# A 128-column memset, and a wait for it, ahead of each table look-up from the thirteenth tile on

## The chip, the cores and the metric

The kernel runs on one core of a Trainium2 chip. The metric is the device time in microseconds (us) of one execution; lower is better. Times in the text are in us unless ns is written.

## What is computed

A recommendation tower for a batch of 1,024 samples. Each sample looks up 32 embedding rows of 64 numbers, one in each of 32 tables. For each of the 496 pairs of fields, one embedding goes through that pair's own 64x64 matrix and is multiplied and summed with the other embedding. The 496 sums and 16 dense features pass three small layers.

```python
e = jnp.stack([tbl_0[ids[:, 0]], ..., tbl_31[ids[:, 31]]], axis=1)      # (1024, 32, 64)
p, q = e[:, ROW], e[:, COL]                                             # the 496 pairs
z = jnp.sum(jnp.einsum('bpj,ipj->bpi', p, kernel) * q, axis=-1)
h = jnp.concatenate([z, dense_ctx], axis=1)
h = jnp.maximum(h @ W_top1 + b_top1, 0.0)
h = jnp.maximum(h @ W_top2 + b_top2, 0.0)
y = h @ W_top3
```

All of it is in float32.

## The kernel before, in words

**Tiles.** The batch is cut into four blocks of 256 samples, the 32 fields into 16 tiles of two fields. So there are 64 tiles, numbered `m` = 0 to 63, sixteen to a block. A tile of one block is 256 samples x 128 numbers (two fields of 64). Tiles 0, 1 and 4 are not looked up by GpSimd (TensorE makes them by a product with one-hot rows), the other 61 are.

**Look-ups.** GpSimd runs one long loop over the tiles (L401 on). A tile takes four look-ups, one for each of two groups of 128 samples and each of two fields. Each is an indirect DMA (L419) that fetches 128 rows of 64 numbers into `nat` (a ring of eight tiles) or `nat01` (the first two tiles of a block). That is 244 look-ups in all. Before a look-up GpSimd may wait for semaphores: for `transposed` (the ring's slot was read by TensorE, once for each tile), and for `u_ready` and `summed`, which count TensorE's progress. The numbers for these last two come from a plan (`PLAN.in_front`), and ask for work that TensorE does some seven and a half tiles ahead of the tile's own turn. They hold GpSimd back from running further ahead; they are the gates of the text below.

**TensorE.** Its order is written out by the class `Plan` ahead of time and doesn't change with what arrives first. It turns a tile (L644, `transpose`: two or, from the second block on, four matmuls against `ident`) once its look-ups have landed (`gathered`). ScalarE copies the result to `rows` (L492). Then come the pieces of the pair work that need this tile: `interact` (L690 and L697) and `interact_pass` (L711), each 8 or 4 matmuls. VectorE multiplies each piece with the other embedding (L607, L618), ScalarE sums some of them (L504), and TensorE sums the others (`add_up`, L724 and L730). From block 1 on tiles are turned two at a time, as pairs 16/17, 18/19, up to 62/63. TensorE waits at L644 if a pair has not landed, and everything behind it in its order waits too. When the last pair is turned, the rest of the pair work and the three layers (L771, L791, L799) follow.

**The look-up next to other GpSimd work.** Apart from the look-ups GpSimd runs only the set-up at the start: a memset of `ident` (L395), an affine select that waits for it (L397), and an iota (L399).

Of the kernel before, what the change touches and what calls it, by code (L numbers as in the profile page):

```python
# [8 lines left out]
P = 128  # L9
# [94 lines left out]
def tile_at(m):  # L104
    b, tile = divmod(m, TILES)
    return b, FRONT[tile] if b == 0 and tile < len(FRONT) else tile
# [16 lines left out]
def lane_count(m):  # L123

    return 32 * SUBS * (m // LANES + (m % LANES not in BY_PRODUCT))
# [2 lines left out]


AHEAD = 30  # L130


def pieces_in_front(m):
    return max(0, (4 * m - AHEAD) * (ND + NP) // (4 * TILES))

# [9 lines left out]
class Plan:  # L145
# [90 lines left out]
    def in_front(self, m, part):  # L236

        first, last = (next(mark[0] for mark in self.marks if mark[1] == n * (ND + NP)) for n in (1, BLOCKS))
        due = first + (last - first) / (4 * (LOOKED_UP - TILES)) * (4 * (m - TILES) - AHEAD + part)
        return max(mark for mark in self.marks if mark[0] <= max(0, due))  # L240
# [54 lines left out]
def tower(nc, ids, first_ids, tables, kern, dense, w1, b1, w2, b2, w3, out):  # L295
    f32, f32r, u32 = mybir.dt.float32, mybir.dt.float32r, mybir.dt.uint32
    ALU, ACT = mybir.AluOpType, mybir.ActivationFunctionType
    with ExitStack() as ctx:
        def sb(name, shape, dt=f32):
            return ctx.enter_context(nc.sbuf_tensor(name, shape, dt))  # L300
# [4 lines left out]
        def sem(name):  # L305
            return ctx.enter_context(nc.semaphore(name))
# [18 lines left out]
        ident = sb("ident", [P, P])  # L325
        row_number = sb("row_number", [P, CHUNKS])
        sel = sb("sel", [P, 62])


        w1_sb, w2_sb = rows[:, :, 0:P], rows[:, 0:HID1 * HID2 // P // P, P:2 * P]  # L330
# [34 lines left out]
        def h_ps(n):  # L365
            return u_flat[:, n % 6, :]

        ids_in, ident_zero, ident_ready = sem("ids_in"), sem("ident_zero"), sem("ident_ready")
        row_number_ready, ones_ready = sem("row_number_ready"), sem("ones_ready")
        distance_ready, ones_by_act = sem("distance_ready"), sem("ones_by_act")  # L370
# [13 lines left out]
        def nat_of(m, s):  # L384

            b, tile = tile_at(m)
            return nat01[:, b % 2, s, tile, :] if tile < 2 else nat[:, m % RING, s, :]
# [5 lines left out]
        @block.gpsimd  # L393
        def _(pool):
            nc.gpsimd.memset(ident[:], 0.0).then_inc(ident_zero, 1)  # L395
            pool.wait_ge(ident_zero, 1)
            nc.gpsimd.affine_select(out=ident[:], in_=ident[:], compare_op=ALU.not_equal, fill=1.0, base=0,  # L397
                                    pattern=[[-1, P]], channel_multiplier=1).then_inc(ident_ready, 1)
            nc.gpsimd.iota(row_number[:], [[1, CHUNKS]], base=0, channel_multiplier=CHUNKS,  # L399
                           allow_small_or_imprecise_dtypes=True).then_inc(row_number_ready, 1)  # L400
            pool.wait_ge(ids_in, 16)  # L401
            for m in range(LOOKED_UP):
                if m in BY_PRODUCT:
                    continue
                b, tile = tile_at(m)
                if m >= LANES:
                    pool.wait_ge(transposed, m - LANES + 1)
                if tile == 0 and b >= 2:
                    pool.wait_ge(prod_ready, AT[b - 2, None, NP - 1] + 1)
                for n in range(SUBS):  # L410
                    for h in range(2):
                        _, pieces, quads = PLAN.in_front(m, 2 * n + h)
                        if pieces:
                            pool.wait_ge(u_ready, pieces)
                        if quads:
                            pool.wait_ge(summed, quads)
                        f = 2 * tile + h
                        col = (b * SUBS + n) * FIELDS + f
                        pool.indirect_dma_start(  # L419
                            nat_of(m, n)[:, h * EMBED:(h + 1) * EMBED], None, tables[f],  # L420
                            bass.IndirectOffsetOnAxis(ids_sb[:, col:col + 1], 0)).then_inc(gathered[m % LANES], 16)
            for m in range(LOOKED_UP - LANES, LOOKED_UP):
                pool.wait_ge(gathered[m % LANES], lane_count(m))
# [428 lines left out]
```

## Time and profile before

| | |
|---|---|
| time, median of 3 runs | 498.26 us |
| lowest and highest of the runs | 494.0 and 500.97 us |
| span of the profiled execution (first to last instruction) | 412.5 us |
| busy in that span: TensorE (PE) | 403.7 us, 98% |
| busy: VectorE (DVE), ScalarE (ACT), GpSimd (POOL) | 298.6, 259.1, 231.6 us |

The span runs from the first to the last instruction on the engines. The measured time also holds what lies around it, 498.26 - 412.5 = 85.8 us if the profiled execution was like the others. A busy TensorE is one whose matmuls lie back to back in the records; their ends are modelled. A look-up's busy time is GpSimd's part in it (making the descriptors of the transfer), not the transfer.

### The profile page before, as it was taken

Reading aid. Unit: us, or ns where it says so; the run is one execution under the profiler, and the core shown is the slowest. Engines: PE = TensorE matmul, PEld = TensorE weight load, DVE = VectorE, ACT = ScalarE, POOL = GpSimd, SP = SyncE. Lnnn points to the kernel's source line nnn. Section 1 sums busy time; section 2 is a strip of 40 time slices with the busy share of each in tenths; the row PEclk is TensorE's granted clock in tenths of the full one; section 3 lists DMA queues with packets and bytes.
Section 4 is the critical chain, followed back from the end, with each engine's and each line's share of the span. In section 5 each row is a group of like instructions: output and inputs, shape, how many; then the busy total and the mean of one; then the engine's idle time right before and its main releaser. Section 6 shows DMA issues by size and latency. Waiting matters only on the chain.

```text
span 412.5 us, 10180 instructions
## 1 busy us (share of the span) xinstructions
PE 403.7 (98%) x3421; PEld 254.4 (62%) x3421; DVE 298.6 (72%) x293; ACT 259.1 (63%) x1874; POOL 231.6 (56%) x251
## 2 busy tenths in 40 slices
PE   7889999999999999999999999999999999999997
PEld 5556656667675766666766665666666566654442
DVE  6776887878788887878979798878879888740000
ACT  6476877667577876764796867719978667002221
POOL 6777777777677757776766777677767200000000
PEclk9998999999999999999999999999999999999999
DMA  6665661131281111211211113111311020000000
GB/s 177 210 200 155 191 221 33 27 77 27 37 219 28 29 19 47 61 28 25 63 42 28 25 25 79 24 27 26 79 25 27 15 51 2 2 2 0 2 0 1
DMA packets 18266, 24.31 MB, mean 59 GB/s; under 512 B 6387, under 2 KB 11767, under 8 KB 17958
## 3 DMA queue, kind: packets, MB, share of 16 engines
q1 hardware_dynamic: 10406, 15.64, 13.0%
q0 software_dynamic: 7808, 8.01, 9.7%
q8 instruction: 28, 0.46, 0.4%
q14 instruction: 24, 0.20, 0.2%
HBM read 19.44 MB, written 0.00 MB: 47 GB/s over the span
## 4 chain that ended last, share of the span: by engine, by line
PE 92%; DMA 3%; POOL 3%; issue 1%; ACT 0%
PE u_ps L690 41%; PE z_ps L724 14%; PE u_ps L711 13%; PE z_ps L730 7%; PE u_ps L771 7%; PE t_ps L644 4%; PE u_ps L791 3%; POOL nat L419 3%; DMA nat<-tbl,ids_sb 2%; PE u_ps L697 2%; DMA ids_sb<-ids 1%; PE t_ps L677 0%; PE u_ps L799 0%; ACT y_sb L571 0%
## 5 line engine op out<-in xcount | busy, mean ns | idle before, releaser
L419 POOL DMA_INDIRECT nat<-tbl,ids_sb x244 | 230.5, 945 | 90.7 <-issue 56.6
L607 DVE TENSOR_TENSOR prod<-u_ps,rows 128x1024 f32<-128x1024 f32 x184 | 213.5, 1218 | 56.7 <-PE u_ps L690 56.7
L504 ACT ACTIVATE pass_prod<-pass_prod 128x64 f32<-128x64 f32 x896 | 214.3, 243 | 22.1 <-DVE pass_prod L618 22.1
L690 PE MATMUL u_ps<-rows,k_sb 64*128 64x256 f32 x1472 | 176.2, 387 | 0.0
L504 ACT ACTIVATION_READ_ACCUMULATOR pass_prod<-pass_prod 128x1 f32 x896 | 169.9, 190 | 0.0
L690 PEld LDWEIGHTS u_ps<-rows,k_sb 64*128 64x128 f32 x1472 | 139.0, 188 | 46.0 <-DVE pass_prod L618 13.4
L618 DVE TENSOR_TENSOR pass_prod<-u_ps,nat 128x1024 f32<-128x1024 f32 x56 | 67.2, 1215 | 1.2 <-PE u_ps L711 1.2
L711 PE MATMUL u_ps<-k_sb,rows 64*128 64x256 f32 x448 | 61.5, 394 | 0.6 <-ACT rows L492 0.6
L724 PE MATMUL z_ps<-prod,sel 128*32 128x512 f32 x512 | 61.6, 598 | 0.0
L492 ACT ACTIVATE rows<-t_ps 128x512 f32<-128x512 f32 (+1 forms) x38 | 19.6, 516 | 54.2 <-PE t_ps L644 54.0
L711 PEld LDWEIGHTS u_ps<-k_sb,rows 64*128 64x128 f32 x448 | 40.6, 186 | 14.6 <-DVE prod L607 9.6
L730 PE MATMUL z_ps<-prod,sel 128*32 128x256 f32 x512 | 30.7, 382 | 0.0
L724 PEld LDWEIGHTS z_ps<-prod,sel 128*32 128x32 f32 x512 | 13.4, 109 | 27.1 <-issue 24.5
L771 PE MATMUL u_ps<-zT,rows 128*128 128x512 f32 x64 | 27.7, 594 | 0.0
L644 PE MATMUL t_ps<-ident,nat 128*128 128x128 f32 x122 | 21.4, 289 | 3.4 <-DMA nat<-tbl,ids_sb 2.8
L730 PEld LDWEIGHTS z_ps<-prod,sel 128*32 128x32 f32 x512 | 15.1, 109 | 12.5 <-issue 2.7
L644 PEld LDWEIGHTS t_ps<-ident,nat 128*128 128x128 f32 x122 | 12.7, 141 | 16.3 <-issue 11.5
L771 PEld LDWEIGHTS u_ps<-zT,rows 128*128 128x128 f32 x64 | 12.1, 190 | 15.2 <-issue 15.2
L562 ACT ACTIVATE k_sb<-u_ps,b_sb 128x512 f32<-128x512 f32 x8 | 5.5, 687 | 22.4 <-PE u_ps L771 22.4
L791 PE MATMUL u_ps<-k_sb,rows 128*128 128x512 f32 x32 | 13.9, 592 | 0.0
L610 DVE TENSOR_TENSOR prod<-u_ps,by_self 128x1024 f32<-128x1024 f32 x8 | 9.8, 1220 | 5.5 <-PE u_ps L697 5.5
L791 PEld LDWEIGHTS u_ps<-k_sb,rows 128*128 128x128 f32 x32 | 6.1, 190 | 7.7 <-issue 7.7
(50 smaller groups left out, 78.9 us busy)
## 6 DMA issues: line engine op xcount, KB each, us to landing
by_self<-rows SPq DMA_DIRECT2D x32, 128.0 KB
nat<-tbl,ids_sb POOLq DMA_INDIRECT x244
k_sb<-kern SPq DMA_DIRECT2D x3, 768.0 KB, 5.6
k_sb<-kern SPq DMA_DIRECT2D x2, 640.0 KB, 5.7
k_sb<-kern SPq DMA_DIRECT2D x1, 1152.0 KB, 5.2
k_sb<-kern SPq DMA_DIRECT2D x2, 512.0 KB
rows<-w SPq DMA_DIRECT2D x1, 1024.0 KB, 6.6
rows<-tbl SPq DMA_DIRECT2D x4, 224.0 KB
```

Of the source, the lines that this page charges most:

```text
L419: pool.indirect_dma_start(nat_of(m, n)[:, h * EMBED:(h + 1) * EMBED], None, tables[f], bass.IndirectOffsetOnAxis(ids_sb[:, col:col + 1], 0 ...
L492: nc.scalar.activation(rows[:, tile:tile + count, cols_of(b)], t_ps[:, 0:count].rearrange("p t n c -> p t (n c)"), ACT.Copy).then_inc(rows ...
L504: op = nc.scalar.activation(of, of, ACT.Copy, accum_out=z_nat[:, b % 2, s, row:row + 1])
L607: nc.vector.tensor_tensor(to, u, by.unsqueeze(1).to_broadcast([P, 2, 2, SIZE]), ALU.mult).then_inc(prod_ready, 1)
L618: nc.vector.tensor_tensor(pass_prod[:, k % CRING], u, by.to_broadcast([P, 2, 2, SIZE]), ALU.mult).then_inc(prod_ready, 1)
L644: op = nc.tensor.transpose(t_ps[:, t, s, :], nat_of(m + t, s), ident[:])
L690: op = nc.tensor.matmul(u[:, h, :], k_sb[part, k_of(d), side, :], rows[part, tile, cols_of(b)], start=True, stop=True)
L711: op = nc.tensor.matmul(u_ps[:, n % URING, h, t, :], rows[part, first + t, at:at + P], k_sb[part, k].rearrange("p s n -> p (s n)"), start= ...
L724: op = nc.tensor.matmul(z_ps[32 * k:32 * k + 32, :, :], sel[:, 30 - 2 * slot:62 - 2 * slot], prod[:, (a + k // 2) % PRING, k % 2], start=s ...
L730: op = nc.tensor.matmul(z_ps[32 * k:32 * k + 32, 0, :], sel[:, 30 - row:62 - row], prod[:, (a + k // 2) % PRING, k % 2, side], start=slot ...
L771: op = nc.tensor.matmul(h_ps(n), w1_sb[:, r * (HID1 // P) + m, :], zT[:, r, cols], start=r == 0, stop=r == ZROWS - 1)
L791: op = nc.tensor.matmul(h_ps(8 + n), w2_sb[:, g * (HID2 // P) + m, :], h1T(g, cols), start=g == 0, stop=g == HID1 // P - 1)
```

## The change

A new tensor `zeros` (128 x 128 float32) and a new semaphore `zeros_there` are added. For tiles with `m >= 12`, in front of each look-up and behind the gates of that look-up, GpSimd writes zeros into `zeros` and waits until that write is complete. Nothing reads `zeros`. Tiles 2, 3 and 5 to 11 (36 look-ups) stay as they were; tiles 12 to 63 (52 tiles, 208 look-ups) have the memset and the wait.

```diff
+SPACED = 12
...
+        zeros = sb("zeros", [P, P])
...
+        zeros_there = sem("zeros_there")
...
                         if quads:
                             pool.wait_ge(summed, quads)
+                        if m >= SPACED:
+                            nc.gpsimd.memset(zeros[:], 0.0).then_inc(zeros_there, 1)
+                            pool.wait_ge(zeros_there, 4 * (m - SPACED) + 2 * n + h + 1)
                         f = 2 * tile + h
                         col = (b * SUBS + n) * FIELDS + f
                         pool.indirect_dma_start(
```

**Where the spacing starts.** The rows below are GpSimd's own instructions in program order around the border from tile 11 to tile 12. A row is the line, the operation, what it writes and reads, the semaphores it waits for, and a count of like instructions in a row. Before:

```order
L419 DMA nat<-tbl,ids_sb 128x64 [waits summed,u_ready,transposed]
L419 DMA nat<-tbl,ids_sb 128x64 [waits summed,u_ready] x3
L419 DMA nat<-tbl,ids_sb 128x64 [waits summed,u_ready,transposed]
L419 DMA nat<-tbl,ids_sb 128x64 [waits summed,u_ready] x3
L419 DMA nat<-tbl,ids_sb 128x64 [waits summed,u_ready,transposed]
L419 DMA nat<-tbl,ids_sb 128x64 [waits summed,u_ready] x3
```

And of the changed kernel (L419 is now L425, the memset is L421):

```order
L425 DMA nat<-tbl,ids_sb 128x64 [waits summed,u_ready,transposed]
L425 DMA nat<-tbl,ids_sb 128x64 [waits summed,u_ready] x3
L421 MEMSET zeros 128x128 [waits summed,u_ready,transposed]
L425 DMA nat<-tbl,ids_sb 128x64 [waits zeros_there]
L421 MEMSET zeros 128x128 [waits summed,u_ready]
L425 DMA nat<-tbl,ids_sb 128x64 [waits zeros_there]
L421 MEMSET zeros 128x128 [waits summed,u_ready]
L425 DMA nat<-tbl,ids_sb 128x64 [waits zeros_there]
L421 MEMSET zeros 128x128 [waits summed,u_ready]
L425 DMA nat<-tbl,ids_sb 128x64 [waits zeros_there]
```

The gates now stand on the memset, and the look-up waits for the memset alone. Before, a look-up whose gates were open had nothing to wait for.

**Block starts.** The same holds further on, at the first tile of the third block, whose look-up had four waits. Here the rows carry the tables' numbers. Before:

```order
L419 DMA nat01<-tbl_0,ids_sb 128x64 [waits u_ready,summed,prod_ready,transposed]
L419 DMA nat01<-tbl_1,ids_sb 128x64 [waits summed,u_ready]
L419 DMA nat01<-tbl_0,ids_sb 128x64 [waits summed,u_ready]
L419 DMA nat01<-tbl_1,ids_sb 128x64 [waits summed,u_ready]
L419 DMA nat01<-tbl_2,ids_sb 128x64 [waits summed,u_ready,transposed]
```

Of the changed kernel:

```order
L421 MEMSET zeros 128x128 [waits u_ready,summed,prod_ready,transposed]
L425 DMA nat01<-tbl_0,ids_sb 128x64 [waits zeros_there]
L421 MEMSET zeros 128x128 [waits summed,u_ready]
L425 DMA nat01<-tbl_1,ids_sb 128x64 [waits zeros_there]
L421 MEMSET zeros 128x128 [waits summed,u_ready]
L425 DMA nat01<-tbl_0,ids_sb 128x64 [waits zeros_there]
```

No look-up has changed its place among the look-ups, and TensorE, VectorE, ScalarE and SyncE have the same instructions in the same order as before.

## Rows read from the trace of the kernel before

**Rows 1.** The page: busy time, and the chain that ended last by engine

```profile
PE 403.7 (98%) x3421; PEld 254.4 (62%) x3421; DVE 298.6 (72%) x293; ACT 259.1 (63%) x1874; POOL 231.6 (56%) x251
PE 92%; DMA 3%; POOL 3%; issue 1%; ACT 0%
```

**Rows 2.** Windows (start:end, length, busy of each engine), two stretches

```profile
core 0: us, PE busy (x) PEld busy (x) DVE busy (x) ACT busy (x) POOL busy (x), PEclk, DMA share, GB/s
48.50:332.60 284.10, 284.10 (x2634) 186.27 (x2630) 236.93 (x207) 205.54 (x1586) 196.18 (x208) 1.00 0.22 50
332.60:412.50 79.90, 77.29 (x480) 40.44 (x478) 27.55 (x24) 21.69 (x111) 0.00 (x0) 1.00 0.03 8
```

**Rows 3.** GpSimd's groups by line: busy us, mean ns, idle before, releasers

```profile
L419 POOL DMA_INDIRECT nat<-tbl,ids_sb x244 | 230.5, 945 | 90.7 <-issue 56.6 <-PE u_ps L690 16.3 <-PE z_ps L724 5.7
```

**Rows 4.** Timeline of GpSimd: tile 11's last look-ups, tile 12's first

```profile
start us, us, engine line op out<-in xcount [idle before <-releaser]
45.99 0.94 POOL L419 DMA_INDIRECT nat<-tbl,ids_sb  x1 [0.30 <-PE u_ps L711]
47.24 0.95 POOL L419 DMA_INDIRECT nat<-tbl,ids_sb  x1 [0.30 <-issue]
48.49 0.94 POOL L419 DMA_INDIRECT nat<-tbl,ids_sb  x1 [0.31 <-issue]
49.73 0.95 POOL L419 DMA_INDIRECT nat<-tbl,ids_sb  x1 [0.30 <-PE u_ps L690]
```

**Rows 5.** The same: last look-up of tiles 17, 59 and 63

```profile
77.20 0.94 POOL L419 DMA_INDIRECT nat<-tbl,ids_sb  x1 [0.30 <-issue]
...
300.80 0.96 POOL L419 DMA_INDIRECT nat<-tbl,ids_sb  x1 [0.31 <-PE u_ps L697]
...
322.22 0.94 POOL L419 DMA_INDIRECT nat<-tbl,ids_sb  x1 [0.55 <-issue]
```

**Rows 6.** Timeline of TensorE: where pairs 16/17, 58/59 and 62/63 are turned

```profile
88.17 0.66 PE L644 MATMUL t_ps<-ident,nat 128*128 128x128 f32 x4
...
305.30 0.66 PE L644 MATMUL t_ps<-ident,nat 128*128 128x128 f32 x4
...
332.65 0.65 PE L644 MATMUL t_ps<-ident,nat 128*128 128x128 f32 x4
```

**Rows 7.** Tile 3: its last look-up, and the weight load (PEld) that waited for it

```profile
12.28 0.94 POOL L419 DMA_INDIRECT nat<-tbl,ids_sb  x1 [0.30 <-issue]
15.63 0.20 PEld L644 LDWEIGHTS t_ps<-ident,nat 128*128 128x128 f32 x2 [0.77 <-DMA nat<-tbl,ids_sb]
```

**Rows 8.** Chain that ended last: two look-ups from start to landing

```profile
17.27 5.88 DMA nat<-tbl,ids_sb
27.26 4.41 DMA nat<-tbl,ids_sb
```

**Rows 9.** Timeline of GpSimd at the start: set-up and first two look-ups

```profile
0.74 0.20 POOL L395 MEMSET ident<- 128x128 f32 x1 [0.29 <-POOLq L808]
1.19 0.64 POOL L397 TENSOR_SCALAR_AFFINE_SELECT ident<-ident 128x128 f32<-128x128 f32 x1 [0.24 <-POOL ident L395]
1.79 0.13 POOL L399 IOTA row_number<- 128x8 f32 x1
3.22 1.27 POOL L419 DMA_INDIRECT nat<-tbl,ids_sb  x1 [1.29 <-DMA ids_sb<-ids]
4.80 0.94 POOL L419 DMA_INDIRECT nat<-tbl,ids_sb  x1 [0.30 <-issue]
```

**Rows 10.** GpSimd's groups again: the set-up's memset, 128 columns

```profile
L395 POOL MEMSET ident<- 128x128 f32 x1 | 0.2, 204 | 0.3 <-POOLq L808 0.3
```

**Rows 11.** Windows: before, in and after a fall of the clock (PEclk)

```profile
26.40:31.70 5.30, 3.26 (x28) 2.44 (x26) 5.23 (x5) 4.22 (x35) 4.08 (x5) 1.00 0.64 183
33.00:36.50 3.50, 3.50 (x21) 2.84 (x20) 2.45 (x2) 3.50 (x31) 2.59 (x4) 0.51 0.55 128
36.50:48.50 12.00, 12.00 (x110) 6.82 (x108) 9.24 (x8) 8.76 (x70) 8.95 (x11) 1.00 0.75 239
```

## The prediction

> **What bounds the kernel now.** I read the page first: TensorE is busy for 98% of the span, and the chain that ended last is 92% TensorE [rows 1]. Then I cut the span in two by windows. Up to 332.6 us GpSimd still looks rows up, and TensorE is busy in every microsecond; behind it come 79.9 us of TensorE work with no look-up left [rows 2]. So TensorE bounds the kernel, and the look-ups cost nothing as long as each pair of tiles has landed by its turn.
>
> How much room is there? The mean share of GpSimd (56%) misleads. A look-up is busy for 0.945 us [rows 3], but back-to-back look-ups start 1.25 us apart, 0.94 busy and 0.30 between [rows 4]. From the first look-up of tile 12 (48.49) to the last of tile 63 (322.22) there are 207 intervals [rows 4, 5]: 273.7 / 207 = 1.322 us each. At full speed they would be 1.25 us. So GpSimd is at 95% of what it can issue, and only 15 us in this stretch are waits for gates. This is the number on which the change falls.
>
> The deadline of each pair is in TensorE's timeline: pairs 16/17, 58/59 and 62/63 are turned at 88.17, 305.30 and 332.65, with nothing waited for [rows 6]. From 16/17 to 62/63 there are 23 steps: 244.5 / 23 = 10.6 us for eight look-ups, 1.33 us for one.
>
> How long after its start can a look-up be used? Tile 3's last one starts at 12.28 and the weight load that waited for it starts at 15.63, which is 3.35 us [rows 7]; two others in the busy early part took 5.88 and 4.41 [rows 8]. Pair 58/59 was turned 4.5 us after its last look-up started, without a wait [rows 5, 6], so it took at most that. I take 3.4 us, because the DMA queues are much quieter later on (share 0.22 against 0.64 [rows 2, 11]). The cushion is then 88.17 - 77.20 - 3.4 = 7.6 us at pair 16/17, 305.30 - 300.80 - 3.4 = 1.1 us at pair 58/59 and 332.65 - 322.22 - 3.4 = 7.0 us at the last pair.
>
> **The change, part by part.** Nothing is removed, and TensorE's order is the same. Added are 208 memsets and 208 waits, all on GpSimd. The only things queued behind the memset are the look-ups, and TensorE waits for these at L644.
>
> The price is the new spacing of look-ups. I build it from four parts.
>
> 1. The look-up's own busy time, 0.94 us [rows 4].
> 2. From its end to the start of the memset. The trace has no memset behind a look-up. From below: an instruction that waits for nothing can start before the one ahead has ended; the iota starts at 1.79 while the affine select runs to 1.83 [rows 9]. So 0. From above: the 0.30 us between two look-ups [rows 4]. I take 0.20: the predecessor is that of the upper row, but part of the 0.30 must belong to the start of the second look-up.
> 3. The memset, 0.204 us for the same 128 x 128 shape [rows 10].
> 4. From its end to the look-up that waits for it. The set-up has the same pattern, a memset and an instruction that waits for it: 0.24 us [rows 9]. The 0.30 in front of a look-up is the other bound. I take 0.27. This wait can't be hidden: it is the point of the semaphore.
>
> The sum is 0.94 + 0.20 + 0.20 + 0.27 = 1.62 us (1.61 before rounding up). The ends are 0.94 + 0 + 0.20 + 0.24 = 1.39 and 0.94 + 0.30 + 0.20 + 0.30 = 1.75 us.
>
> One rule bears on step 3. A start-to-start reading of the set-up gives 1.19 - 0.74 = 0.45 us from the memset to the instruction waiting for it [rows 9], against 0.20 + 0.24 = 0.44 as I add it. The Trainium skill (Perfetto Trace Analysis, the part on the GPSIMD engine instruction) says that a GpSimd span is unreliable and should be timed by start-to-start spacing. By that alone the period would be 1.25 + 0.45 = 1.70 us and the time about 570 us; the row agrees with the span to 0.01 us, so this moves only step 2 to its upper end.
>
> Now the schedule. The last unspaced look-up starts at 47.24 [rows 4]. The k-th spaced one starts at 47.24 + 1.62 k if it never waits for a gate. Eight look-ups take 13.0 us where TensorE wants a pair each 10.6 us. Each look-up loses 1.62 - 1.25 = 0.37 us. The cushion of 7.6 us at pair 16/17 is used up after some 20 look-ups, about there; from pair 18/19 on TensorE waits at nearly each pair.
>
> - Tile 59 ends with spaced look-up 4 x 48 = 192: it starts at 47.24 + 311.0 = 358.3 instead of 300.80, 57.5 us later. Less 1.1 us of cushion: TensorE turns the pair 56.4 us later.
> - Tile 63 ends with number 208: 47.24 + 337.0 = 384.2 instead of 322.22, 62.0 us later, less 7.0: 55.0 us. The earlier pair decides.
>
> The gates cost nothing more. They ask for TensorE's work of some seven tiles earlier, and TensorE will stand waiting for the next pair when GpSimd gets to them, so it has done everything ahead of that. The 15 us of gate waits of before vanish into the spacing; the sum above has them, since it goes by start times. The tail of 79.9 us [rows 2] is unchanged and moves as a whole.
>
> So the span goes from 412.5 to 412.5 + 56.4 = 468.9 us. The median of the runs, 498.26, is 85.8 us above the profiled span; the same 56.4 us on it gives 554.7, **555 us**, 11% slower. Each 0.1 us on the spacing is worth 19.2 us.
>
> **The rivals.**
>
> *A: the memset hides, and the time stays.* It runs beside the end of the look-up ahead, and the dependent look-up is dispatched at once. The turning point is where tile 59 uses only its cushion: 47.24 + 192 p = 300.80 + 1.1, p = 1.326 us; up to p = 1.38 the loss is under 10 us, 2%. At 1.326 the time would be 498, at 1.38 some 508 us. For it: GpSimd's starts do overlap once [rows 9]. Against it: even with step 2 at zero, the rows give 1.39. The Trainium skill (GPSIMD Engine Reference, Instruction dispatch) says that consecutive GpSimd instructions are no barrier between its eight cores, and that one instruction's completion waits for all eight. By this most cores could write zeros early, but those that made the descriptors could not, and the wait is for all; so the rule allows step 2 to be short and not the sum to be under 1.39, some 510 us. No row here shows the cores apart.
>
> *B: a look-up behind another kind of instruction starts cold.* The first look-up, behind the iota, was busy for 1.27 us, the second for 0.94 [rows 9]: 0.33 more. If each memset has this effect, the spacing is 1.95 us: 47.24 + 192 x 1.95 = 421.6, 120.8 us later, less 1.1: 119.7, and 618 us. Against it: the first look-up is also the first of the program, and the row can't say which of the two it was.
>
> *C: TensorE falls to its lower clock while it waits.* After a stretch of 5.3 us in which it was busy for 3.26, it ran at a granted clock of 0.51 (1.2 GHz) for 3.5 us, then at 1.00 again [rows 11]. In the changed kernel it idles 2.4 us in every 13.0. If each pair brought one such fall, its 10.6 us of work would grow by some 1.7 us to 12.3, still under 13.0: the waits get shorter and nothing is lost. Only a fall behind the last wait counts, 1.7 us or so. It would have to last through whole pairs to decide, and then there would be no idle time left to cause it. As an addition above 10 us I give it little.
>
> *D: faster.* Look-ups that are further apart could land sooner, or leave more for the other transfers. The transfers behind 48.5 us hold up nothing now [rows 2], so there is nothing to win.
>
> **How the numbers follow.** Chances: the forecast's mechanism with a spacing from 1.39 to 1.80 us 0.82 (510 to 589 us), A 0.05, B 0.10, C as a large addition 0.02, D 0.01. Low end: a spacing of 1.43 gives 47.24 + 274.6 - 300.80 - 1.1 = 19.9, 518 us. High end: 1.82 gives 94.5, 593 us; this is a little above the rows' upper bound, and takes in a small part of B. Beyond these I leave one in ten above and less than one below. About 2% is what a measurement of this kernel can tell from no change. Faster by more than 2%: 0.01; within 2%: 0.05; slower: 0.94.
>
> **What would show it.** In GpSimd's timeline behind 48 us: a memset of 0.20 us in front of each look-up, starts 1.62 us apart (1.39 to 1.75), with idle time of about 0.2 and 0.27 on its two sides, and no gate named as a releaser behind pair 18/19. TensorE waits at L644 for the look-ups' DMA, some 2.4 us at each of about 23 pairs, 56 us in all, and is busy for 86% of the span rather than 98%. The chain that ended last runs through GpSimd from about 50 to 360 or 380 us. The last look-up starts near 384, and the stretch behind the last turn is still about 80 us. I am wrong if look-ups keep their 1.25 us apart, if their busy time changes from 0.94, or if the tail grows.

## The result, and the profile after

In the same comparison the kernel before took 497.15 us and the changed kernel 500.99 us (medians of 20 runs each). The ratio is 1.0067, with a 95% interval from 1.0039 to 1.0096; it is taken from the executions within 1.5% of each kernel's fastest. I had said 555 us, with 518 to 593 as the range. Both the size and the range were wrong: the change costs some 3 to 4 us there and not 57.

The experiments found which step failed, and one fact has to stand first. **Comparisons of this kernel come in two kinds.** A comparison here is one session, in which the kernels run in turn on one chip. In some, every execution of the kernel before takes 488 to 503 us; in others every one takes 411 to 417 us, with nothing between. I call them the long and the short kind. The profile from which I predicted has a span of 412.5 us, so it is of the short kind. The times beside it, 498.26 us as the median, are of the long kind. I took the 85.8 us between them for time that lies around the span. In the changed kernel's profiled run the time is 504.66 us and the span 502.9, so what lies around it is 1.8 us.

The changed kernel in the long kind, its page:

```profile
span 502.9 us, 10388 instructions
PE 438.3 (87%) x3421; PEld 262.3 (52%) x3421; DVE 302.2 (60%) x293; ACT 261.2 (52%) x1874; POOL 277.5 (55%) x459
PE 72%; another core or an unknown queue 10%; DVE 7%; ACT 6%; issue 4%; DVEq 0%; ACTq 0%
L425 POOL DMA_INDIRECT nat<-tbl,ids_sb x244 | 231.7, 949 | 95.5 <-issue 40.0
L421 POOL MEMSET zeros<- 128x128 f32 x208 | 44.7, 215 | 37.2 <-PE u_ps L696 12.9
```

TensorE was 98% busy in [rows 1] and is 87% busy here, as I had expected (86%), and yet not for my reason. The 208 memsets are there, 215 ns each. In front of them GpSimd still waits for TensorE (`u_ps L696`): it is held by the gates, so it is not the bound.

Its spacing where no gate holds it, from GpSimd's timeline:

```profile
67.56 0.95 POOL L425 DMA_INDIRECT nat<-tbl,ids_sb  x1 [0.27 <-POOL zeros L421]
68.52 0.22 POOL L421 MEMSET zeros<- 128x128 f32 x1
69.01 0.95 POOL L425 DMA_INDIRECT nat<-tbl,ids_sb  x1 [0.27 <-issue]
```

Look-ups start 1.44 us apart: 0.95 busy, next to nothing to the memset, 0.22 for it, 0.27 behind it. Before it was 1.25 us [rows 4].

TensorE's waits at the turning of tiles (all of line L650, from the view of one line):

```profile
L650 PE MATMUL t_ps<-ident,nat x122: 272/273/475, 29.2 to 423.4; 128*128 128x128 f32 x122
its engine sat idle before it (us, times) until:
  ACT rows L498: 0.8, 1
```

TensorE never sits idle at a turn for a look-up, where I had forecast 56 us of such waits. The last of these matmuls starts at 423.4. And the cut of the span by windows, which answers to [rows 2]:

```profile
48.50:423.00 374.50, 326.31 (x2756) 201.44 (x2754) 252.33 (x218) 222.06 (x1700) 251.71 (x426) 0.97 0.20 47
423.00:502.90 79.90, 77.30 (x480) 40.45 (x478) 27.53 (x24) 20.44 (x99) 0.00 (x0) 1.00 0.03 8
```

The tail is 79.9 us in both. All of the difference between the kinds lies in the part in which look-ups run, and there TensorE is no longer busy in every microsecond (326.3 of 374.5).

### The profile page after: what moved, and what is told of

Its sections match the earlier page's. It is cut to its first block, busy times and chain, and to the rows that moved or that the text cites. A ratio compares the mean times of both kernels' runs of the same rounds, so it can differ in the third digit from the quotient of the medians.

```text
span 502.9 us, 10388 instructions
## 1 busy us (share of the span) xinstructions
PE 438.3 (87%) x3421; PEld 262.3 (52%) x3421; DVE 302.2 (60%) x293; ACT 261.2 (52%) x1874; POOL 277.5 (55%) x459
## 4 chain that ended last, share of the span: by engine, by line
PE 72%; another core or an unknown queue 10%; DVE 7%; ACT 6%; issue 4%; DVEq 0%; ACTq 0%
PE u_ps L696 31%; PE z_ps L730 12%; PE u_ps L717 12%; DVE prod L613 6%; PE u_ps L777 6%; PE z_ps L736 4%; PE t_ps L650 3%; ACT pass_prod L510 3%; PE u_ps L797 3%; DVE pass_prod L624 1%; PE u_ps L703 1%; PE z_ps L672 1%; ACT rows L498 1%; PE t_ps L683 0%
## 5 line engine op out<-in xcount | busy, mean ns | idle before, releaser
L425 POOL DMA_INDIRECT nat<-tbl,ids_sb x244 | 231.7, 949 | 95.5 <-issue 40.0
L696 PE MATMUL u_ps<-rows,k_sb 64*128 64x256 f32 x1472 | 186.7, 391 | 37.4 <-DVE prod L613 27.8
L696 PEld LDWEIGHTS u_ps<-rows,k_sb 64*128 64x128 f32 x1472 | 138.9, 187 | 94.2 <-DVE prod L613 43.7
L717 PE MATMUL u_ps<-k_sb,rows 64*128 64x256 f32 x448 | 69.3, 436 | 9.3 <-DVE prod L613 6.9
L421 POOL MEMSET zeros<- 128x128 f32 x208 | 44.7, 215 | 37.2 <-PE u_ps L696 12.9
L717 PEld LDWEIGHTS u_ps<-k_sb,rows 64*128 64x128 f32 x448 | 44.8, 208 | 30.2 <-DVE prod L613 18.6
L736 PE MATMUL z_ps<-prod,sel 128*32 128x256 f32 x512 | 34.2, 382 | 1.4 <-issue 1.1
L730 PEld LDWEIGHTS z_ps<-prod,sel 128*32 128x32 f32 x512 | 13.5, 110 | 28.8 <-issue 28.1
L736 PEld LDWEIGHTS z_ps<-prod,sel 128*32 128x32 f32 x512 | 16.4, 109 | 16.0 <-issue 7.1
L650 PE MATMUL t_ps<-ident,nat 128*128 128x128 f32 x122 | 22.6, 299 | 0.9 <-ACT rows L498 0.8
L650 PEld LDWEIGHTS t_ps<-ident,nat 128*128 128x128 f32 x122 | 13.2, 145 | 14.6 <-issue 14.6
L672 PE MATMUL z_ps<-zT,rows 125*64 125x256 f32 x16 | 6.0, 567 | 9.1 <-issue 9.0
```

Source lines behind the costliest of these rows:

```text
L421: nc.gpsimd.memset(zeros[:], 0.0).then_inc(zeros_there, 1)
L425: pool.indirect_dma_start(nat_of(m, n)[:, h * EMBED:(h + 1) * EMBED], None, tables[f], bass.IndirectOffsetOnAxis(ids_sb[:, col:col + 1], 0 ...
L650: op = nc.tensor.transpose(t_ps[:, t, s, :], nat_of(m + t, s), ident[:])
L696: op = nc.tensor.matmul(u[:, h, :], k_sb[part, k_of(d), side, :], rows[part, tile, cols_of(b)], start=True, stop=True)
L717: op = nc.tensor.matmul(u_ps[:, n % URING, h, t, :], rows[part, first + t, at:at + P], k_sb[part, k].rearrange("p s n -> p (s n)"), start= ...
L730: op = nc.tensor.matmul(z_ps[32 * k:32 * k + 32, :, :], sel[:, 30 - 2 * slot:62 - 2 * slot], prod[:, (a + k // 2) % PRING, k % 2], start=s ...
```

## The experiments

### The kernel before and the changed kernel once more (e1, e2)

> The kernel before, unchanged, with a profile. Theory S (the profiled execution of before was not typical; in the timed ones TensorE is held up while look-ups run, and the measured time is the span plus about 2 us, as in the changed kernel): span about 495 us, time about 497 us, look-ups back to back 1.25 us apart but with long waits for gates, tail behind the last turn 80 us. Theory F (85 us lie around the span in every execution of before): span about 412 us and time about 497 us.

> The changed kernel, unchanged, a second profile. Both theories: spacing 1.44 us where no gate is waited for. S: span about 499 us, time about 501 us, no wait for look-ups at TensorE's turns behind tile 12. F: the first profile was the odd one; span about 434 us (412.5 + 21.8, from 192 look-ups at 1.44 us) and time about 520 us.

Measured: the kernel before 491.94 us (ratio to itself 0.9993, 0.9949 to 1.0037), its profiled span 493.2. The changed kernel 493.71 us, ratio 1.0030 (0.9986 to 1.0075), its span 491.1. So theory S holds and F has fallen: in this comparison the time is the span plus some 2 us, and the first profile of before was of something else. The kernel before, its page, the chain that ended last, two places in TensorE's timeline and the windows:

```profile
span 493.2 us, 10180 instructions
PE 438.9 (89%) x3421; PEld 262.6 (53%) x3421; DVE 301.9 (61%) x293; ACT 261.0 (53%) x1874; POOL 232.0 (47%) x251
PE 78%; another core or an unknown queue 7%; DVE 7%; issue 5%; ACT 3%; POOL 0%; DVEq 0%; POOLq 0%; ACTq 0%
...
113.40 0.66 PE L644 MATMUL t_ps<-ident,nat 128*128 128x128 f32 x4
...
413.42 0.66 PE L644 MATMUL t_ps<-ident,nat 128*128 128x128 f32 x4
...
48.50:413.40 364.90, 326.81 (x2758) 201.94 (x2754) 252.53 (x218) 220.69 (x1691) 206.11 (x218) 0.96 0.19 48
```

Pairs 16/17 and 62/63 are turned at 113.40 and 413.42, against 88.17 and 332.65 in [rows 6]. That is 300.0 us for 184 look-ups, 1.63 us each; in the first profile it was 1.33. At a pace of 1.63 us a spacing of 1.44 us fits in beside it.

The two spans differ by 80.7 us: 25.2 us have come up by the turn of pair 16/17, 55.5 more by that of 62/63, and nothing behind it. TensorE has the same 3,421 matmuls. It is idle for 54.3 us instead of 8.8, and busy for 438.9 us instead of 403.7, so 35 of the 80.7 us are in matmuls that take longer. A part of this is the clock, whose mean over the span is 0.952 here and was 0.996. It is not all: e15 below, of the short kind, has a mean clock of 0.941 and TensorE busy for 425.7 us.

### More memsets, in the long kind (e3, e4, e11)

```diff
-                            nc.gpsimd.memset(zeros[:], 0.0).then_inc(zeros_there, 1)
-                            pool.wait_ge(zeros_there, 4 * (m - SPACED) + 2 * n + h + 1)
+                            for x in range(2):
+                                nc.gpsimd.memset(zeros[:], 0.0).then_inc(zeros_there, 1)
+                                pool.wait_ge(zeros_there, 2 * (4 * (m - SPACED) + 2 * n + h) + x + 1)
```

(four instead of two in e4)

> Two memsets in front of each look-up from the thirteenth tile on, each waited for. Spacing 1.44 + 0.49 = 1.93 us. S: TensorE's own pace in the changed kernel is (423 - 116) / (23 x 8) = 1.67 us per look-up, so GpSimd becomes the bound: the last look-up starts near 65 + 208 x 1.93 = 466 us, 56 us later than in the changed kernel, less about 9 us of cushion: time near 548 us. A variant of S in which TensorE is held up by the look-ups themselves: the same or less, 535 to 548. F: (1.93 - 1.44) x 192 = 94 us on top of the changed kernel.

> Four memsets in front of each look-up, each waited for. Spacing 1.44 + 3 x 0.49 = 2.91 us; the last look-up starts near 65 + 208 x 2.91 = 670 us. All theories: GpSimd bounds, time near 670 + 4 + 80 = 754 us. If TensorE's stalls come from the look-ups, they are hidden in its waits here, and TensorE's work between two waits should take about the 10.6 us of the first profile again, plus stalls.

> Two memsets in front of each look-up again (spacing 1.70 us as measured in e3_two). Where the kernel before takes 412 us, GpSimd bounds throughout: tile 59's last look-up starts at 47.2 + 192 x 1.71 = 375.5, 74.7 us later than before, less a cushion of 2.1: 72.6 us more, time about 485 us, 47 us above the changed kernel (438). Where the kernel before takes 492 us: about 506 us, as in e3_two.

Measured: two memsets 506.54 us, ratio 1.0298 (1.0220 to 1.0376), and again in another comparison of the long kind 506.29 against 494.83 us, ratio 1.022 (1.0091 to 1.035), where I had expected 506. Four memsets 615.22 us, a single run. My first expectations of 548 and 754 us were far too high. The reason is in the timeline of GpSimd, here with four and then with two memsets:

```profile
153.11 0.95 POOL L426 DMA_INDIRECT nat<-tbl,ids_sb  x1 [0.27 <-POOL zeros L422]
154.06 1.00 POOL L422 MEMSET zeros<- 128x128 f32 x4
155.33 0.95 POOL L426 DMA_INDIRECT nat<-tbl,ids_sb  x1 [0.27 <-POOL zeros L422]
```

```profile
159.40 0.95 POOL L426 DMA_INDIRECT nat<-tbl,ids_sb  x1 [0.27 <-POOL zeros L422]
160.36 0.48 POOL L422 MEMSET zeros<- 128x128 f32 x2
161.11 0.95 POOL L426 DMA_INDIRECT nat<-tbl,ids_sb  x1 [0.27 <-POOL zeros L422]
```

The spacing is 2.22 and 1.71 us. A further memset with its wait adds 0.26 us, not the 0.49 that I had taken: the 0.27 us stands before the look-up alone, and a memset that waits for a memset starts almost at once. At 1.71 us GpSimd has passed TensorE's 1.63, and TensorE waits at the turns:

```profile
L651 PE MATMUL t_ps<-ident,nat x122: 272/300/476, 28.2 to 425.8; 128*128 128x128 f32 x122
its engine sat idle before it (us, times) until:
  issue: 52.1, 15
```

This is 52.1 us in 15 waits in e3, but the last turn is only 12 us later than in e1 (425.8 against 413.8 for the last matmul). So most of what TensorE loses elsewhere in e1 must lie within these waits. The step from 1.63 to 1.71 over 184 look-ups would be 15 us, and the measured medians differ by 14.8 (506.54 - 491.72).

That GpSimd sets the pace here is seen best beside e15, the same kernel in the short kind. Where pairs 16/17 and 62/63 are turned, e3 and then e15:

```profile
107.23 0.63 PE L651 MATMUL t_ps<-ident,nat 128*128 128x128 f32 x4 [0.29 <-issue]
...
425.40 0.65 PE L651 MATMUL t_ps<-ident,nat 128*128 128x128 f32 x4
```

```profile
90.22 0.63 PE L651 MATMUL t_ps<-ident,nat 128*128 128x128 f32 x4 [4.51 <-issue]
...
408.69 0.55 PE L651 MATMUL t_ps<-ident,nat 128*128 128x128 f32 x3
```

The stretch takes 318.2 us in the long kind and 318.5 us in the short one. The kinds differ only ahead of it, by 17.0 us.

### Look-ups left out, and the second kind of comparison (e5, e6, e7)

The holds of TensorE might come from the look-ups themselves. From tile 18 on, three (e5) or two (e6) of the four look-ups of a tile are left out, and the counts that TensorE waits for are lowered to fit. In e7, as in e5, three are left out, and four memsets with waits stand in the place of each:

```diff
+                        if m >= FULL and (n, h) not in KEPT:
+                            continue
                         f = 2 * tile + h
```

> The kernel before, with three of four look-ups left out from tile 18 on (the fourth, of the second group of samples and the second field, stays, with its gates), so part of the data is stale. TensorE has the same instructions. Theory L (the look-ups themselves hold up TensorE and VectorE in the ordinary executions): behind pair 18/19 TensorE comes back towards the 10.6 us per pair of the first profile, from some 13.1; 22 pairs x 2.5 = 55 us less, time about 437 us. Theory N (the holds have nothing to do with look-ups): time about 492 us, 13 us per pair.

> The same with two of four look-ups left out. L: between the two, about 465 us. N: about 492 us.

> As e5_quarter, and each look-up left out is replaced by four memsets of 128 columns with their waits (some 1.05 us), so GpSimd is as busy as before but moves a quarter of the rows. If the transfers or the making of descriptors hold up TensorE: as e5_quarter, 437 us by theory L. If GpSimd being busy does it: about 492 us. N: about 492 us.

Measured: 412.14, 412.25 and 412.71 us. But in this comparison the kernel before took 412.1 us as well (21 runs, 411.4 to 414.65), and the ratios are 0.9991 (0.9970 to 1.0012), 1.0005 (0.9986 to 1.0025) and 1.0024 (1.0005 to 1.0044). So these three say nothing on the holds: there were none to take away. They say something else. Where the kernel before takes 412 us the look-ups cost it nothing, and it is bound by TensorE, as I had read.

### The wait taken from the look-up (e8)

```diff
-                            nc.gpsimd.memset(zeros[:], 0.0).then_inc(zeros_there, 1)
-                            pool.wait_ge(zeros_there, 4 * (m - SPACED) + 2 * n + h + 1)
+                            if (m, n, h) != (SPACED, 0, 0):
+                                pool.wait_ge(zeros_there, 4 * (m - SPACED) + 2 * n + h)
+                            nc.gpsimd.memset(zeros[:], 0.0).then_inc(zeros_there, 1)
```

> The changed kernel with the wait moved: the memset waits for the memset before it, and the look-up waits for nothing but its gates. If the 0.27 us behind the memset is the price of the wait, the spacing of free look-ups falls from 1.44 to at most 1.3 us; if it is the look-up's own start, it stays 1.44. Time within 1% of the changed kernel either way, since in ordinary executions GpSimd is not the bound at 1.44.

Measured, in the same comparison of the short kind: 421.05 us, ratio 1.0212 (1.0166 to 1.0258). GpSimd's timeline:

```profile
100.33 0.95 POOL L426 DMA_INDIRECT nat<-tbl,ids_sb  x1 [0.17 <-POOL zeros L423]
101.28 0.22 POOL L423 MEMSET zeros<- 128x128 f32 x1
101.66 0.95 POOL L426 DMA_INDIRECT nat<-tbl,ids_sb  x1 [0.17 <-POOL zeros L423]
```

The spacing is 1.33 us. So of the 0.27 us behind the memset, 0.10 is the wait, and 0.17 is there without it. The memset itself adds only 0.08 us to the 1.25 of two look-ups in a row [rows 4], since its 0.22 us comes with a gap of 0.17 where there was one of 0.30. Neither of my two values, at most 1.30 or 1.44, was met, and the time is not within 1% of the changed kernel's either, which takes 438.21 us in the short kind (e9). That 1.33 us, TensorE's own pace there, already costs about 2% shows how little room there is. Not all of it is the spacing: at 1.33 us the last look-up of tile 59 would start at 302.6, and it starts at 309.85, because a few look-ups come later than that, as the one at 122.10, which is 3.09 us behind its predecessor.

### Both kernels in the short kind (e9, e10)

> The changed kernel again, to have it beside the kernel before where that takes 412 us. Look-ups 1.44 us apart, as measured. If the kernel before takes about 412 us in this comparison (TensorE's pace 1.33 us per look-up): GpSimd bounds; tile 59's last look-up starts at 47.24 + 192 x 1.44 = 323.7, 22.9 us later than before; landing takes 2.4 us and not 3.4 (so the cushion is 2.1): 20.8 us more, time about 433 us, +5%. If the kernel before takes about 492 us (pace 1.63): the same as before within 1%.

> The kernel before with a profile, in the same comparison. Where it takes 412 us: TensorE busy in every microsecond of the look-up stretch, pairs turned at 88 and 333 us. Where it takes 492 us: at about 113 and 413 us, with holds of 0.7, 1.4 and 2.1 us in TensorE's stream.

Measured: the changed kernel 438.21 us against 412.23, ratio 1.0632 (1.0601 to 1.0663). The kernel before beside it gave 413.18, ratio 1.0006 (0.9974 to 1.0038), its profiled span 410.0. I had expected 433 us. The changed kernel's rows: its page, GpSimd's timeline at the start and at tile 59, TensorE's at pairs 58/59 and 62/63, and the waits at the turns:

```profile
span 436.7 us, 10388 instructions
...
47.15 0.95 POOL L425 DMA_INDIRECT nat<-tbl,ids_sb  x1 [0.30 <-issue]
48.09 0.22 POOL L421 MEMSET zeros<- 128x128 f32 x1
48.58 0.95 POOL L425 DMA_INDIRECT nat<-tbl,ids_sb  x1 [0.27 <-POOL zeros L421]
...
161.63 0.96 POOL L425 DMA_INDIRECT nat<-tbl,ids_sb  x1 [1.53 <-issue]
...
327.09 0.96 POOL L425 DMA_INDIRECT nat<-tbl,ids_sb  x1 [0.27 <-PE u_ps L717]
...
329.52 0.63 PE L650 MATMUL t_ps<-ident,nat 128*128 128x128 f32 x4 [2.63 <-issue]
...
356.84 0.66 PE L650 MATMUL t_ps<-ident,nat 128*128 128x128 f32 x4
...
PE t_ps L650 <- issue: 18.6, 8, 5.5
PE t_ps L650 <- DMA nat<-tbl,ids_sb: 2.6, 1, 2.6
```

Here the mechanism of the forecast is seen whole. Tile 59's last look-up starts at 327.09 instead of 300.80 [rows 5], 26.3 us later. TensorE stands still for 2.63 us and turns the pair at 329.52, 24.2 us later than in [rows 6]; the last pair follows at 356.84, 24.2 us later as well. GpSimd names no gate for more than a moment (at most 0.3 us behind tile 12).

The kernel before in the same comparison (e10) turns the same two pairs 2.4 us earlier than the first profile did:

```profile
302.87 0.66 PE L644 MATMUL t_ps<-ident,nat 128*128 128x128 f32 x4
...
330.22 0.66 PE L644 MATMUL t_ps<-ident,nat 128*128 128x128 f32 x4
```

Against these the changed kernel is 26.6 us later, and the medians differ by 26.0 (438.21 - 412.23). In e10 TensorE is busy in every microsecond from 48.5 to the last turn (281.7 us), as I had expected.

### The crossing, and the look-ups left out in the long kind (e12 to e15)

> The kernel before with three of four look-ups left out from tile 18 on, as e5_quarter (part of the data is stale). Where the kernel before takes 412 us: 412 us, as there. Where it takes 492 us: theory L (the holds of TensorE come with the look-ups) says about 437 us; theory N (they don't) says 492 us.

> As e7_quarter_busy: three of four look-ups left out from tile 18 on and each replaced by four memsets with waits, so that GpSimd is as busy and moves a quarter of the rows (part of the data is stale). Where the kernel before takes some 492 us: if the transfers or the making of their descriptors bring the holds, 440 us as e12_quarter_again; if GpSimd being busy brings them, about 492 us. Where it takes 412 us: 412 us.

> As e6_half: two of four look-ups left out (part of the data is stale). Where the kernel before takes some 492 us: halfway in the number of look-ups (each one left out is worth (493 - 440) / 138 = 0.38 us, and here 92 are left out), about 458 us. Where it takes 412 us: 412 us.

> Two memsets in front of each look-up. Where the kernel before takes 412 us: 485 us, as reckoned for e11_two_again. Where it takes some 492 us: 506 us, as measured twice.

e12 fell in a comparison of the long kind, with e11: the kernel before took 494.83 us, and with three of four look-ups left out from tile 18 on it took 440.14, ratio 0.8885 (0.8774 to 0.8995). Theory L had said 437. The page, windows and line of e12:

```profile
span 439.1 us, 10042 instructions
...
48.50:359.70 311.20, 303.26 (x2762) 195.67 (x2758) 250.12 (x218) 220.11 (x1694) 75.68 (x80) 0.99 0.16 42
...
121.89 0.66 PE L649 MATMUL t_ps<-ident,nat 128*128 128x128 f32 x4
...
L649 PE MATMUL t_ps<-ident,nat x122: 272/273/476, 28.4 to 359.7; 128*128 128x128 f32 x122
```

Pair 18/19 is turned at 121.89 and the last pair at 359.27, 237.4 us later: 10.8 us for each of 22 pairs. That is the pace of the short kind (e10 takes the same 237.4 us, from 92.84 to 330.22), and not the 13.1 us of e1 (from 125.30 to 413.42). TensorE's instructions are the same. So in the long kind the stops of TensorE go when the look-ups go, and 54.7 us of time with them; in the short kind the same look-ups cost nothing.

e13 and e14 fell in a comparison of the short kind: 412.12 and 412.25 us against 412.33, ratios 0.9999 (0.9974 to 1.0024) and 0.9994 (0.9964 to 1.0023). Again there was nothing to take away.

e15 was in the same comparison: two memsets, 489.91 us, ratio 1.189 (1.1815 to 1.1964). I had expected 485. With e9 it gives the price of spacing in the short kind: from 1.44 to 1.71 us, 489.91 - 438.21 = 51.7 us for 0.27 x 192 = 51.8. Against the kernel before, two memsets cost 77.6 us in the short kind and 11.5 and 14.8 us in the long one.

### More attempts on what holds TensorE (e16 to e18)

> As e13_busy_again. Where the kernel before takes some 492 us: 440 us if the transfers or the making of their descriptors bring the holds, about 492 us if a busy GpSimd brings them. Where it takes 412 us: 412 us again (part of the data is stale).

> As e14_half_again. Where the kernel before takes some 492 us: about 458 us if the holds go by the number of look-ups. Where it takes 412 us: 412 us again (part of the data is stale).

> As e16_busy_third: where the kernel before takes some 492 us, 440 us if the transfers or the making of their descriptors bring the holds, about 492 us if a busy GpSimd brings them. Where it takes 412 us: 412 us again (part of the data is stale).

Both comparisons were of the short kind, with 412.88 and 412.11 us for the kernel before. Measured: 412.56, 412.42 and 412.66 us, ratios 0.9992 (0.9968 to 1.0015), 0.9999 (0.9979 to 1.0020) and 1.0007 (0.9977 to 1.0037). So it stays open whether in the long kind the transfers hold TensorE or a busy GpSimd does, and whether it goes by the number of look-ups.

### What the traces of the long kind leave out

There is a third candidate, on which the traces that we have say something. A trace also holds the updates of semaphores, by which the profile finds what released a wait. For the same kernel these are 5,927 in e10 and 2,979 in e1. By stretch, with the time at which it ends (us):

| stretch | e10, short | e1, long | e5, short, look-ups left out | e12, long, look-ups left out |
|---|---|---|---|---|
| up to the turn of pair 18/19 | 1,941 (92.8) | 844 (125.3) | 1,819 (93.7) | 874 (121.9) |
| from there to the turn of 62/63 | 3,551 (330.2) | 1,700 (413.4) | 1,560 (331.1) | 1,485 (359.3) |
| behind it | 435 | 435 | 437 | 437 |

Where e1 and e12 have stops, half or more of the updates are missing against e10 and e5; where they have none (the end of both, and e12 behind pair 18/19), nearly all are there. Two things follow. First, in the long kind a wait that the profile puts down to "issue" or to "another core or an unknown queue" (7% of e1's chain, none of e10's) can be one whose update isn't in the trace. Second, the recording of the updates may itself be what holds the engines. The look-ups bring most of them: with 138 look-ups fewer, e5 has 2,111 updates fewer than e10, some 15 each. But it may as well be that one other cause both stops the engines and loses the updates. No run here decides it, and none shows an execution that was not recorded.

The times of one kernel by kind, in one table (medians, us):

| | spacing | long kind | short kind |
|---|---|---|---|
| before | 1.25 | 491.7, 491.9, 494.8, 497.2 | 412.1 to 413.2 |
| memset, wait not on the look-up (e8) | 1.33 | not run | 421.1 |
| the change | 1.44 | 493.7, 501.0 | 438.2 |
| two memsets | 1.71 | 506.5, 506.3 | 489.9 |
| four memsets | 2.22 | 615.2 (one run) | not run |
| TensorE's pace per look-up in the kernel before | | 1.63 | 1.33 |

## Why the prediction was wrong

**The step that failed most** is the one on the span and the median: "The median of the runs, 498.26, is 85.8 us above the profiled span; the same 56.4 us on it gives 554.7". The 85.8 us do not lie around the span; 1.8 us do. The rest lies inside it, ahead of the last turn, as TensorE's stops and slower matmuls, as e1 shows. With them the pace of TensorE is 1.63 us per look-up and not 1.33, and this number decides whether a slower GpSimd is felt. With the measured spacing of 1.44 us but this step as it was, I would have said 520 us, still 19 too many. A profile that is 16 to 18% shorter than the timed runs can't be of the same circumstances. I saw the gap, named it, and did not ask what it would do to the cushions. Had I spread the 85.8 us evenly over the 244 look-ups, some 0.35 us each, TensorE's pace would have come out as 1.68 us by this estimate. Even my spacing of 1.62 us lies below that and below the 1.63 of e1: no change within 2%.

**What bounds the kernel** was right for the short kind (e10: pairs and tail as in the first profile; e5 and e6: nothing gained by fewer look-ups). In the timed runs TensorE is the slower of the two as well, but its stream has stops that go when look-ups go (e12). So look-ups are not free there, and the 7.6, 1.1 and 7.0 us of cushion don't hold.

**The spacing** was forecast as 1.62 us and is 1.44. Step 1 was 0.94 and is 0.95. Step 2, from the look-up's end to the memset, was 0.20 and is nothing: the memset starts 0.94 us behind the look-up's start (47.15 and 48.09 in e9). This was the lower of my bounds. Of the sum for the spacing it is the term that was mis-sized, and it alone accounts for 0.18 x 192 = 35 of the 56.4 us: the row that I took as nearest, the gap of 0.30 us between two look-ups, belongs to the start of the second one (0.17 of it is still there in front of a look-up in e8). Step 3 was 0.20 and is 0.22; step 4 was 0.27 and is 0.27. The start-to-start reading of the set-up, by which the time would have been 570 us, was further off than the sum of spans: its 0.45 us holds (0.49 here), but the gap that I left in the 1.25 beside it does not.

**The landing** was taken as 3.4 us after the start and is 2.4 (327.09 to 329.52 in e9, where TensorE was waiting). So the cushion at pair 58/59 is 2.1 us and not 1.1.

**The schedule** holds where the profile holds. With 1.44 for the spacing my sum gives 47.24 + 276.5 - 300.80 - 1.1 = 21.8 us. The run has 24.2: 1.0 less for the larger cushion, and 3.4 more for look-ups that came later than 1.44 us apart, among them two waits of 1.53 us that nothing in the profile explains, as at 161.63. That pair 58/59 decides, that the gates add nothing and that the tail moves as a whole was all seen in e9; in the short kind the change costs 6.3% where I had said 11%. TensorE waits for look-ups 9 times there, 21.2 us in all and up to 5.5 us at once, not at nearly every pair. And the chain that ended last doesn't run through GpSimd, as I had said it would: it is 93% TensorE, 5% issue and 0% GpSimd. Two of the prediction's figures are off by a little: at 1.38 us the loss is 10.3 us and not under 10, and at 1.82 it is 94.8 and not 94.5.

**Rival A**, that the time stays, was right in its result for the timed runs, and wrong in its reason: the memset doesn't hide in the look-up ahead, since the spacing grew by 0.19 us. What hid it was the slower pace of TensorE. I gave it 0.05, because I had let the short profile fix the turning point at 1.33 to 1.38 us. What the Trainium skill (GPSIMD Engine Reference, Instruction dispatch) says, no barrier between consecutive instructions on GpSimd's cores and a completion that waits for all of them, allows step 2 to be zero, and the trace has it at zero. The look-up that waits for the completion starts 0.27 us behind the memset, so the sum stays above its floor of 1.39, at 1.44.

**Rival B**, a cold start of each look-up, is out: all 244 of them in the changed kernel have a mean of 949 ns, against 945 in [rows 3]. **Rival C**, the clock, happened in e9 and mattered little. After 5.6 us of waiting TensorE ran at the lower level for 6.3 us:

```profile
115.30:120.90 5.60, 0.05 (x3) 0.04 (x1) 1.85 (x2) 0.53 (x5) 4.51 (x9) 0.96 0.83 215
120.90:127.20 6.30, 6.30 (x28) 4.58 (x28) 2.45 (x2) 2.61 (x17) 5.21 (x9) 0.50 0.41 95
```

The next pairs' waits can take that up, and the total follows GpSimd's starts. In the timed runs the lower clock is a part of TensorE's slower pace, but of both kernels alike: its mean is 0.952 to 0.979 in every execution of e1 and e2. **Rival D** did not occur.

**Not settled.** Of the 0.67% in the first comparison and the 0.30% in e2 (an interval that reaches below 1) I have no cause; at no turn does TensorE sit idle there for a look-up. Nor is it known what makes a comparison long or short, or what stops TensorE in the long kind. It is not the chip's number: a chip numbered 4 was long once and short once. What I can say is that a comparison stayed of one kind throughout.

## What to carry to other kernels

Before costing anything, hold the profile's span against the timed runs. If the gap between them is larger than what can lie around a kernel, the profile is of other circumstances; then every cushion read from it is uncertain by the whole gap, and the range has to hold the case in which the gap lies inside. An operation added to an engine that runs ahead costs little up to the pace of the engine that consumes (3 to 4 us at 1.44 of 1.63 us, 9 us right at the pace in e8), and its full time multiplied by the number of steps beyond it: find both paces and see where the new spacing falls. Where a trace holds far fewer semaphore updates than another of the same kernel, don't read the releasers that it names. For an instruction between two others, take the gap from the instruction that starts, not from the one that ended.

## What the runs showed of the hardware that I had not expected

**Stops that come with look-ups.** In the long kind TensorE's stream has stops, and for most of them its trace names nothing that it waits for. The first are at the start, where TensorE makes a tile by its product. The kernel before in e1 (long) and then in e10 (short), TensorE's timeline over the same 16 matmuls or their beginning:

```profile
12.89 0.59 PE L666 MATMUL z_ps<-zT,rows 125*64 125x256 f32 x2
14.46 0.38 PE L666 MATMUL z_ps<-zT,rows 125*64 125x256 f32 x1 [0.97 <-DVE k_sb L596]
15.15 0.38 PE L666 MATMUL z_ps<-zT,rows 125*64 125x256 f32 x1 [0.32 <-issue]
16.56 0.58 PE L666 MATMUL z_ps<-zT,rows 125*64 125x256 f32 x1 [1.03 <-DVE k_sb L596]
...
20.75 0.58 PE L666 MATMUL z_ps<-zT,rows 125*64 125x256 f32 x1 [1.41 <-issue]
22.86 0.59 PE L666 MATMUL z_ps<-zT,rows 125*64 125x256 f32 x1 [1.52 <-issue]
```

```profile
12.87 1.89 PE L666 MATMUL z_ps<-zT,rows 125*64 125x256 f32 x16
```

The 16 matmuls start at 12.9 in both. They take 1.9 us in e10, and are not done by 22.9 us in e1, where one follows another by 0.69 us (14.46 to 15.15), 1.41 (15.15 to 16.56) or 2.11 (20.75 to 22.86). "issue" means that the engine waited for nothing that the profile shows, and in this trace half of the semaphore updates are missing. Leaving out 138 look-ups took 54.7 us away in e12 and nothing in e5, so in the long kind a look-up costs TensorE 0.4 us on the mean, and no wait in the profile names it.

**A memset on GpSimd is cheap behind a look-up.** It starts with the look-up's end, takes 0.22 us for 128 columns, and shortens the gap in front of the next look-up from 0.30 to 0.17 us where that doesn't wait for it (e8). A second one with its wait adds 0.26 us (e3, e4).
